# Single-head layers: the gate's columns held stationary, its rows normalised by ScalarE, the values' bias added to the rows by GpSimd

## The reference

```
x = x + tanh(g_xattn[0]) * attention_1head(layernorm(x), ctx)
x = x + tanh(g_ffn[0])   * moe_topk_per_expert(layernorm(x))    # 8 experts + a shared one
... layers 1 and 2: 16 heads, a spectral and a ternary feed-forward part
x = x + tanh(g_xattn[3]) * attention_1head(layernorm(x), ctx)
x = x + tanh(g_ffn[3])   * moe_top1(layernorm(x))               # 8 experts
```

## Time and profile before

| | us |
|---|---|
| median of 3 runs | 856.42 |
| lowest, highest | 853.69, 858.28 |
| the profiled execution's own time | 854.72 |
| its span | 852.8 |
| PE busy | 808.8 (95%) |
| VectorE busy | 475.8 (56%) |
| ScalarE busy | 307.2 (36%) |
| GpSimd busy | 264.1 (31%) |

### The profile page before, as it was taken

The page is one execution under the profiler, slowest core; times in us unless marked ns, Lnnn a source line. Parts: engine busy times, 40 slices in busy tenths (PEclk is TensorE's granted clock), DMA queues, the critical chain, the costliest instruction groups (busy, mean ns, idle before and its releaser), DMA issues.

```text
span 852.8 us, 14986 instructions
## 1 busy us (share of the span) xinstructions
PE 808.8 (95%) x5678; PEld 625.0 (73%) x5678; DVE 475.8 (56%) x1269; ACT 307.2 (36%) x610; POOL 264.1 (31%) x352
## 2 busy tenths in 40 slices
PE   8999999999999998899999999869999999999996
PEld 7875675688888886566667666545777777888885
DVE  3784875500132317787888888876998886100000
ACT  3345112213222225454454445435454434322221
POOL 1121333020334322122325313215886124321212
PEclk9999999999999999999999999999999998999999
DMA  8143801035656348000000000000000012464542
GB/s 249 26 149 102 321 2 53 26 95 213 188 178 194 113 109 311 1 2 2 1 2 2 2 2 1 2 2 0 2 2 1 36 39 83 144 203 129 196 134 22
DMA packets 35202, 71.10 MB, mean 83 GB/s; under 512 B 10419, under 2 KB 25147, under 8 KB 30268
## 3 DMA queue, kind: packets, MB, share of 16 engines
q1 hardware_dynamic: 28265, 60.46, 20.0%
q0 software_dynamic: 6144, 8.31, 5.1%
q10 hardware_dynamic: 722, 1.39, 0.4%
HBM read 55.50 MB, written 14.80 MB: 82 GB/s over the span
## 4 chain that ended last, share of the span: by engine, by line
PE 80%; DVE 9%; ACT 4%; issue 3%; DVEq 2%; POOL 1%; DMA 1%; POOLq 0%; SPq 0%; ACTq 0%
PE banks L690 74%; DVE small L2139 3%; ACT arena L1626 2%; ACT arena L1611 1%; PE banks L1303 1%; PE banks L837 1%; PE banks L1128 1%; DVE arena L2188 1%; PE banks L1259 1%; PE banks L1054 1%; PE banks L786 1%; DVE arena L1736 1%; DMA ident<-in_ident 1%; DVE x L2170 0%; ACT arena L1408 0%
## 5 line engine op out<-in xcount | busy, mean ns | idle before, releaser
L690 PE MATMUL banks<-arena 32*120 32x256 f32 (+6 forms) x1848 | 166.6, 375 | 8.3 <-DVE small L2139 4.6
L690 PEld LDWEIGHTS banks<-arena 32*120 32x120 f32 (+5 forms) x1848 | 105.7, 162 | 42.7 <-issue 19.3
L1408 ACT ACTIVATE arena<-banks 128x512 f32<-128x512 f32 (+3 forms) x151 | 79.7, 552 | 132.9 <-PE banks L1201 34.5
L690 PE MATMUL banks<-ffw,arena 128*128 128x256 f32 (+2 forms) x640 | 118.1, 340 | 0.2 <-DVE x L1714 0.2
L690 PE MATMUL banks<-arena,ew 128*128 128x256 f32 x512 | 113.2, 379 | 0.7 <-ACT arena L1408 0.7
L690 PE MATMUL banks<-ew,arena 128*128 128x256 f32 x512 | 113.3, 379 | 0.0
L690 PEld LDWEIGHTS banks<-arena,ew 128*128 128x128 f32 x512 | 97.2, 190 | 14.3 <-ACT arena L1408 1.1
L690 PEld LDWEIGHTS banks<-ew,arena 128*128 128x128 f32 x512 | 96.2, 190 | 12.5
L690 PEld LDWEIGHTS banks<-ffw,arena 128*128 128x128 f16 (+1 forms) x640 | 84.7, 135 | 25.4 <-issue 4.3
L2139 DVE TENSOR_REDUCE small<-banks 128x16 f32<-128x1920 f32 x32 | 69.0, 2156 | 25.9 <-PE banks L690 24.9
L1626 ACT ACTIVATE arena<-banks,mcol 120x2048 f32<-120x2048 f32 x32 | 63.1, 1972 | 42.7 <-PE banks L690 42.7
(11 more groups left out here) (255 smaller groups left out, 1261.7 us busy)
## 6 DMA issues: line engine op xcount, KB each, us to landing
ew<-in_w SPq DMA_DIRECT2D x32, 1024.0 KB, 7.3
xrow<-arena SPq DMA_DIRECT2D x1, 2064.0 KB, 22.4
zrow<-arena SPq DMA_DIRECT2D x8, 256.0 KB, 2.2
ffw<-in_shared SPq DMA_DIRECT2D x2, 1024.0 KB, 7.1
acc<-x SPq DMA_DIRECT2D x4, 512.0 KB, 3.7
ffw<-in_tern SPq DMA_DIRECT2D x2, 1024.0 KB, 7.6
out<-x SPq DMA_DIRECT2D x8, 256.0 KB, 2.0
arena<-xrow SPq DMA_DIRECT2D x7, 258.0 KB, 4.0
```

The lines of the kernel that those rows point to most:

```text
L690: return pe.matmul(o, l, r, start=a, stop=b)
L1408: return nc.scalar.activation(o, i_, ACT.Copy)
```

## The change

- Logits: the gate's 8 columns, padded with zeros to 32, are stationary, and the transposed rows move, 64 columns at a time, in four groups of 32 PSUM partitions. VectorE brings the result back with a transpose of 32x32 blocks.
- The gate's rows of batches 0 to 5 (`LEFT = 6`) are normalised by ScalarE as scale x + bias; GpSimd makes the bias, -mean times rstd, in two more operations after its pow.
- The values are copied by ScalarE, without bias, at the end of `take_k`. The bias row, scaled by the tanh of the layer's gate, is added to x by GpSimd (`add_bias_row`), after the attention's normalisation has read x and before `add_output` adds to it.

```diff
+LEFT = 6
-        gates = sb("gates", [P, 2, KC, E], F32)
+        gates = sb("gates", [P, 2, KC, 32], F32)
...
+            sp.wait_ge(su["consts"], 1)
+            sp.dma_start(gates[:, :, :, 0:E], d["gates"]).then_inc(load["base"], 16)
...
+            g.memset(gates[:, :, :, :], 0.0)
             g.drain().then_inc(su["consts"], 1)
...
@@ GpSimd, one_gate
                 def rstd_of(q, k, a):
                     g.wait_ge(q["var"], b0 + k + 1)
+                    if q is gt and k >= 1:
+                        g.wait_ge(gt["z"], b0 + k)
+                    m = g.tensor_tensor(rstd[:, 2 * a:2 * a + 2], ve[:, 2 * a:2 * a + 2], mhalf[:, 0:2], ALU.pow)
+                    if q is gt and k < LEFT:
+                        g.drain()
+                        for t in range(TB):
+                            m = g.tensor_scalar(nb2[:, t:t + 1], mv[:, 2 + t, 0:1], rstd[:, 2 + t:3 + t], -1.0, ALU.mult, ALU.mult)
+                    m.then_inc(q["rstd"], 1)
+                def add_bias_row(k):
+                    r = rows[:, ROWS.index("v0" if L == 0 else "o3"), :]
+                    g.wait_ge(one["z"], b0 + k + 1)
+                    for t in range(2 * k, 2 * k + TB):
+                        m = g.tensor_tensor(x[:, t, :], x[:, t, :], r, ALU.add)
+                    m.then_inc(one["xo"], 1)
                 if L == 0:
                     rstd_of(one, 0, 0)
+                    g.wait_ge(load["values"], 32)
+                    g.wait_ge(su["tanh"], 1)
+                    r0 = rows[:, ROWS.index("v0"), :]
+                    g.tensor_scalar(r0, r0, tg[:, 0:1], None, ALU.mult)
+                    g.drain()
+                add_bias_row(0)
                 for s in range(NB + 1):
                     if s + 1 < NB:
                         rstd_of(one, s + 1, 0)
...
                     if 1 <= s:
                         rstd_of(gt, s - 1, 1)
+                    if s + 1 < NB:
+                        add_bias_row(s + 1)
...
@@ PE, logits(k)
-                    for t in range(TB):
-                        for c in range(KC):
-                            l = zT_all[:, c, k * SQ + t * P:k * SQ + (t + 1) * P] if L == 0 else zT2[:, k % 2, c, t * P:(t + 1) * P]
-                            m = mm(psum[7][:, t * E:(t + 1) * E], l, gates[:, L // 3, c, :], c == 0, c == KC - 1)
+                    for c in range(KC):
+                        turned = zT_all[:, c, k * SQ:(k + 1) * SQ] if L == 0 else zT2[:, k % 2, c, :]
+                        quarter = turned.rearrange("p (t j i) -> p j t i", t=TB, i=32)
+                        for j in range(4):
+                            m = mm(psum[7][32 * j:32 * j + 32, 0:TB * 32].rearrange("p (t i) -> p t i", t=TB),
+                                   gates[:, L // 3, c, :], quarter[:, j], c == 0, c == KC - 1)
...
@@ ScalarE, end of take_k(k)
+                    if k >= 2:
+                        act.wait_ge(q["y_ps"], b0 + k - 1)
+                    copy(V1[0:SK, k % 2, :], psum[k % 2][0:SK, 256:512]).then_inc(q["V_sb"], 1)
+                def gate_rows(k):
+                    act.wait_ge(gt["rstd"], b0 + k + 1)
+                    if k >= 2 and L == 0:
+                        act.wait_ge(gt["zT_ps"], k - 1)
+                        act.wait_ge(gt[f"stored{k % 2}"], 16 * (k // 2))
+                    for t in range(TB):
+                        dst = zx[:, 2 * k + t, 0:D] if L == 3 else z2[:, 2 * (k % 2) + t, :]
+                        m = nc.scalar.activation(dst, x[:, 2 * k + t, :], ACT.Identity, bias=nb2[:, t:t + 1],
+                                                 scale=rstd[:, 2 + t:3 + t])
+                    m.then_inc(gt["z"], 1)
...
@@ ScalarE, main
                         if 1 <= s <= NB:
                             take_p(s - 1)
+                        if 2 <= s < LEFT + 2:
+                            gate_rows(s - 2)
                         if s + 1 < NB:
                             take_k(s + 1)
...
@@ the row o3, once
-            copy(rows[:, ROWS.index("o3"), :], psum[7][:, 0:D]).then_inc(su["col_sb"], 1)
+            nc.scalar.activation(rows[:, ROWS.index("o3"), :], psum[7][:, 0:D], ACT.Copy, scale=tg[:, 3:4]).then_inc(su["col_sb"], 1)
...
@@ VectorE
                 def stats(q, k, a):
+                    if q is gt and k >= 1:
+                        v.wait_ge(gt["rstd"], b0 + k)
...
-                def take_values(k):
-                    v.wait_ge(one["KT_sb"], b0 + k + 1)
-                    if k >= 2:
-                        v.wait_ge(one["y_ps"], b0 + k - 1)
-                    V.tensor_tensor(V1[0:SK, k % 2, :], psum[k % 2][0:SK, 256:512], rows[0:SK, ROWS.index("v0" if L == 0 else "o3"), :],
-                                    ALU.add).then_inc(one["V_sb"], 1)
...
+                    v.wait_ge(one["xo"], b0 + k + 1)
                     v.wait_ge(one["y_ps"], b0 + k + 1)
...
-                    V.tensor_copy(logit[:, 2 * k:2 * k + 2, :], psum[7][:, 0:TB * E].rearrange("p (t e) -> p t e", t=TB))\
+                    V.transpose(logit32[:, 2 * k:2 * k + 2, :].rearrange("p t e -> p (t e)"), psum[7][:, 0:TB * 32])\
-                        if 2 <= s < NB + 2:
+                        if LEFT + 2 <= s < NB + 2:
+                            v.wait_ge(gt["z"], b0 + s - 2)
                             normalize(gt, s - 2, 1, z2)
```

More of the change, by code:

```diff
@@ L90, in flamingo_kernel @@
         mcol = sb("mcol", [P, 2, NB], F32)
+        nb2 = sb("nb2", [P, TB], F32)
+        logit32 = sb("logit32", [P, NT, 32], F32)
+        logit = logit32[:, :, 0:E]
         class Cut:
@@ L234, in flamingo_kernel @@
         rs = c.take(4 * HC, "p (b h) -> p b h", b=4)
-        logit = c.take(NT * E, "p (t e) -> p t e", t=NT)
         prob = c.take(NT * E, "p (t e) -> p t e", t=NT)
@@ L290, in kv @@
             return 5 if v <= 1 else 6
-        one = sems("one", f"{ln_names} K_ps KT_sb V_sb s_ps nmax p_sb pT_ps pT_sb y_ps x")
+        one = sems("one", f"{ln_names} K_ps KT_sb V_sb s_ps nmax p_sb pT_ps pT_sb y_ps x xo")
         multi = sems("multi", f"{ln_names} q_ps q_sb K_ps K_sb V_ps V_sb s_ps max mq mT_ps mT_sb sT_ps p_exp "
@@ L313, in _ @@
             sp.dma_start(x[:, 4:, :], d["x"][:, 4:, :]).then_inc(load["x"], 16)
-            sp.dma_start(gates[:, :, :, :], d["gates"]).then_inc(load["base"], 16)
+            sp.wait_ge(su["consts"], 1)
+            sp.dma_start(gates[:, :, :, 0:E], d["gates"]).then_inc(load["base"], 16)
             sp.dma_start(headmask[:, :], d["headmask"]).then_inc(load["base"], 16)
@@ L448, in rstd_of @@
                     g.wait_ge(q["var"], b0 + k + 1)
-                    g.tensor_tensor(rstd[:, 2 * a:2 * a + 2], ve[:, 2 * a:2 * a + 2], mhalf[:, 0:2], ALU.pow).then_inc(q["rstd"], 1)
+                    if q is gt and k >= 1:
[12 more added lines that the diff above has]
+                    m.then_inc(one["xo"], 1)
                 if L == 0:
                     rstd_of(one, 0, 0)
+                    g.wait_ge(load["values"], 32)
[4 more added lines that the diff above has]
+                add_bias_row(0)
                 for s in range(NB + 1):
@@ L1836, in main @@
                          .then_inc(su["krow"], 1)
-                        v.wait_ge(load["values"], 32)
                         v.wait_ge(su["tanh"], 1)
-                    take_values(0)
                     for s in range(NB + 3):
@@ L1864, in main @@
                             add_output(s - 1)
-                        if s + 1 < NB:
-                            take_values(s + 1)
                         if L == 3 and s == 6:
```

## The result

The kernel after takes 859.12 us (median of 20 runs), the kernel before 856.12 beside it: ratio of the two 1.004, interval 1.0022 to 1.0057. A second set on another chip gave 858.61 against 853.91, ratio 1.0047 (1.0020 to 1.0074). Of the 20 runs of each kernel one is far longer (996.77 of after, 4643.47 of before), and the ratio leaves it out. So the kernel after is slower by 3 to 5 us, by the ratios inside the 0.5% that the prediction set as the line, and inside its range.

The account below looks back on a forecast made before the run. PE was taken as the bound, then a new loop through GpSimd and VectorE (7.26 us). Layer 0 +3.5 and layer 3 +0.5 gave +4.0 on 854.72: 858.7, plus 1.70 to the median: 860.4, range 853.5 to 867.

Parts of the forecast that it names:

- Logits: PE's logits block: 0.43 us instead of 0.90, 0.47 less per batch, 7.5 for 16 if all on the path.
- PE is the bound by itself: Layer 0 of the kernel before: PE alone sets the step of 6.32 us, with no idle time noted.
- The values' copy: ScalarE's copy waits for the output product, so PE stands 1.06 us before logits; PE's layer 0 step becomes 6.91.
- The new loop: GpSimd's attention rstd queues behind gate's variance and bias rows; loop through GpSimd and VectorE 7.26 us, above PE's 6.91.
- Layer 0: First single-head layer: 0.8 for the first wait, 3.8 for four longer steps, less 0.2 and 0.9: +3.5 us.
- Layer 3: Last single-head layer: longer steps, but the 1.92 wait and the low clock behind it go: +0.5 us in all.
- contention: Layer 3: VectorE's three operations choosing the experts slow down beside GpSimd's row adds: 1.0 us, bounds 0 and 1.5.
- Rival 1: Low clock comes in PE's new gaps, 4.0 us per fall: 864.4 with one, 868.4 with two; chance 22%.
- Rival 2: PE's relief counts in full in layers 0 and 3, new waits hidden by slack: 844.4 us; chance 12%.
- Rival 3: The loop is short (nb2 at its least) and layer 3 has no contention: +1.4 or less, 857.8; chance 12%.
- Rival 4: The logits' column groups don't overlap: 1.8 us per block, +0.9 per batch, about 866; chance 4%.
- The change of mode: PE's tiling changes twice per batch; drains held within the row's 0.12; a whole pass each would lose the logits' saving.

Follow-up runs that it names:

- e5: The kernel before with the new form of the logits alone: 851.25 us, ratio 0.9981 to the kernel before.
- e1: The kernel after with ScalarE's copy of the values put behind gate's copy and the exponentials of the same step: ratio 1.0081 to the kernel before.
- e2: The kernel after with GpSimd's bias rows put behind the rstd of the next attention batch: ratio 1.006 to the kernel before.
- e9: The kernel after with the values' part undone (bias and copy by VectorE), leaving new logits and gate's rows on ScalarE: ratio 1.0053 to the kernel before.
- e3: The kernel after with values' copy last on ScalarE and bias rows behind the rstd on GpSimd: ratio 1.0044 to the kernel before.
- e6: The kernel after with values' copy last on ScalarE, bias rows behind the rstd, and gate's rows back on VectorE: ratio 1.0026 to the kernel before.
- e7: The kernel after with values' copy last, bias rows behind the rstd, output product before gate's transposes on PE, logits one step later: ratio 1.0064 to before.
- e8: The kernel before with the new logits and ten unread products in PE's wait for batch 4 in layer 3: 850.32 us, ratio 0.9931 to before.
- e4: The kernel after with gate's rows normalised by VectorE as before, no -mean*rstd on GpSimd: ratio 1.0047 to the kernel before.
- the first four variants: e1 to e4, four edits of the kernel after run on one chip: ratios 1.0081, 1.006, 1.0044 and 1.0047 to the kernel before.

## Why the prediction was right, point by point

The number held: 860.4 foretold, 859.12 measured; +4.0 on the sum, +3.0 between the medians. The loop that it named is what binds. The +3.0 mixes executions with and without low clock; between the two that the forecast was about, before's profile with low clock in layer 3 and after's without, it is +2.6. The sum for layer 0 is nearer than its terms, and that part is luck. By its steps:

- **Logits.** 0.43 foretold, 0.43 measured. Right; in PE's order the block takes 0.36 (53.39 to 53.75). Its worth was overrated: 0.47 per batch was reckoned as PE's path; e5 shows 0.17 in layer 0 and none in layer 3. "PE is the bound by itself" was wrong: the earlier trace rows showed VectorE with 0.16 of idle time. Over two steps of before, 12.90, VectorE waits for PE once, 0.38, so it has 6.26 to do per step, and e5's step is 6.29. I took one step for the mean (6.32), where before alternates between 6.35 and 6.55.
- **The values' copy.** 1.06 of wait before logits foretold, 0.96 measured; that it lies inside the GpSimd loop is shown by e1, that it binds next at 6.9 by e2.
- **The new loop.** 7.26 foretold, 7.01 to 7.05 measured, and 6.93 once, where the values' copy binds: -mean*rstd 0.45 for 0.60, bias 1.37 for 1.44. Shown by e1 and e2 together. The 2.22 taken for VectorE ends, in the earlier trace rows, at the start of the values' operation (45.79) and not at the end of the output's (45.63); the same stretch is 2.23 in after (51.72 to 53.95), so nothing hangs on it. But I wrote that the rows on ScalarE are not in the loop. They make a second one, 6.93 alone (e9), which I did not see; undoing the bias loop (e3) therefore gains 0.4 per step and not 1.2. The number came out because the longest of three near loops was the one that I had added up.
- **Layer 0.** +3.5 foretold, +3.07 measured. Near, but by two errors that offset each other: from batch 0 to 5 it was to be 0.8 + 3.8 = 4.6 and is 3.28, for before's steps there are not 6.32 but 6.55, 6.35, 6.55 and 5.94; and of the 1.1 that the last two batches were to give back 0.21 shows up to the last transposes.
- **Layer 3.** +0.5 foretold, -0.79 measured. The wait of 1.92 and the low clock behind it went, as said. Up to batch 5's transposes it was to be +0.5 and is -1.31; in the two steps behind them, where nothing was put, it is +0.52. The step from batch 4 to 5 was to be 7.8 and 1.0 for contention; it is 7.33 and 7.35 in the two profiles. The mis-sized term is that 1.0: the operations that choose were not held, for they were all but over when GpSimd's bias rows began, as VectorE and GpSimd show in the kernel after:

```profile
707.36 0.21 DVE L1820 TENSOR_TENSOR arena<-logit,small 128x48 f32<-128x48 f32 x1
707.65 0.21 DVE L1822 SCALAR_TENSOR_TENSOR arena<-arena,tokt 128x48 f32<-128x48 f32 x1
...
708.23 0.24 DVE L1826 TENSOR_TENSOR small<-arena,small 128x48 bf16<-128x48 f32 x1
```

```profile
708.38 1.41 POOL L467 TENSOR_TENSOR x<-x,rows 128x256 f32<-128x256 f32 x2
```

  The choosing stands before batch 4's transposes (709.69). In the step to batch 5 itself two operations on the slots of the chosen experts were held beside the next bias rows. VectorE and GpSimd in after, then VectorE in before, where GpSimd adds none:

```profile
715.77 0.79 DVE L1847 TENSOR_SCALAR arena<-small,tg 128x6 f32<-128x6 f32 x1
716.64 0.60 DVE L1853 TENSOR_TENSOR small<-small,arena 128x6 int32<-128x6 f32 x1
```

```profile
715.81 1.41 POOL L467 TENSOR_TENSOR x<-x,rows 128x256 f32<-128x256 f32 x2
```

```profile
705.19 0.23 DVE L1806 TENSOR_SCALAR arena<-small,tg 128x6 f32<-128x6 f32 x1
705.49 0.17 DVE L1812 TENSOR_TENSOR small<-small,arena 128x6 int32<-128x6 f32 x1
```

  That is 0.99, the size foretold, at another place: they stand behind batch 5's statistics, and batch 5's transposes, which wait for ScalarE's rows, don't feel it. Whether it is part of the +0.52 behind them is not shown. At the normalisation it is 0.43 (e6).
- **Rival 1**, a fall of the clock in the new gaps. None came between the steps with the 0.96 wait, in either layer of either profile. One of 10.2 us came in the first profile at 63.2, 2.8 behind the last such wait of layer 0, and none in the second. It cost 3 (48.61 against 45.40), where 4.0 was put. Low clock of 3.4 us stands at the same place, 61 to 66, in e1, e6, e7, e8 and e9, with and without the new waits: the place is shown, the cause is open.
- **Rival 2** fell: before's step has at most 0.2 to give in layer 0 and nothing in layer 3 before the next thing binds (e5). **Rival 3**, +1.4 or less, had its conditions fulfilled: -mean*rstd near its lower bound and no contention in the loop. The second profile of after, +2.6 in span, lies midway between it and the forecast of +4.0. **Rival 4** is excluded by the 0.43.
- **The change of mode.** The whole block of logits is 0.43, of which I had allowed 0.19 for both ends. The Trainium skill, TensorEngine Tiling (Array Packing), Tiling Modes, Key Properties, has the array drained at a change of mode. The trace shows no drain by itself; if there is one, it is within the 0.43.
- **VectorE beside GpSimd.** e6's pair lost 0.43 and ended just behind the bias rows (46.29 against 46.14). The Trainium skill, SBUF — State Buffer, Who interferes with whom, names the normalisation's kind of operation among those that can take the port pair that the two engines share; the engine that comes second is blocked for the whole of the other's instruction. The trace agrees at that place. The choosing of experts met the bias rows in e4 alone: of its five operations the last took 0.62 where it takes 0.24 in after, and ended at 704.30, the bias rows at 704.24.

```profile
703.68 0.62 DVE L1826 TENSOR_TENSOR small<-arena,small 128x48 bf16<-128x48 f32 x1 [0.43 <-issue]
```

```profile
702.82 1.42 POOL L467 TENSOR_TENSOR x<-x,rows 128x256 f32<-128x256 f32 x2
```

## What to carry to other kernels

Relief for one engine pays only up to the next engine or loop: here VectorE's own work and three loops through GpSimd and ScalarE lie between 6.2 and 7.05 us a step, and an engine that "has room" adds its latency to a loop. Before an operation is moved, list every cycle that passes through its new queue, with the operation's own input in it; the longest decides. And a wait can be cheaper when it is filled than when it is moved: with the new logits, ten products that nobody reads took the ratio from 0.998 to 0.993 (on two chips), where the whole change made it 1.004.

## What the runs showed of the hardware

- On the chip of the first four variants the kernel before had a median of 864.5, against 853.9 to 856.1 on the others, and in all four profiles VectorE stood two or three times, in or behind the last steps of layer 3, for a releaser that the profile does not know. The kernel before was not profiled there. In e3, VectorE and then PE:

```profile
729.17 0.25 DVE L1814 STREAM_TRANSPOSE logit<-banks 128x64 f32<-128x64 f32 x1 [2.55 <-remote]
...
736.48 0.18 DVE L1838 TENSOR_SCALAR arena<-banks 128x16 f32<-128x16 f32 x1 [5.80 <-remote]
```

```profile
730.85 0.52 PE L716 MATMUL banks<-small,ones 128*128 128x16 bf16 x15
```

The product that L1838 reads was done at 731.4, five microseconds earlier. Late instructions are one reading; no run tests it. It stays open.
- A product of one row with 256 columns in fp32, two records: 0.52 of PE's order. Four records of 128 rows with 256 columns take 0.96: by the record one row costs what 128 rows do.
- Low clock (1.2 for 2.4 GHz) costs by the work that stands in it: 6.8 us cost 1.8, 10.2 us 3.6 to 3.9 in layer 3 and about 3 at the end of layer 0.
- PE's unfilled wait for the choosing in layer 3, and the low clock that began within 2 us behind it: before 1.92 and 10.2, twice; e5 2.35 and 6.8; e6 2.62 and 3.4; e9 1.64 and 3.4; e4 1.65 and none; e3 1.25 and none. The longer wait was not followed by the longer fall.
